# Three taps of a depthwise 3x3 convolution as diagonal matmuls on TensorE, among the windows of a window attention

## The reference

```
x = _ln2d(x0, ln_w, ln_b)
x1 = lax.conv_general_dilated(x, dw_w, (1, 1), ((1, 1), (1, 1)), feature_group_count=c, ...) + dw_b
ca = _eca(x1, ...)                                  # gate per channel, from the mean of x1
q, k, v = three 1x1 convolutions of x; v is multiplied by ca
for each head (8 channels): windows of 8x8 pixels, shifted by 4; head 1's k and v are halved by a 2x2 convolution
    atn = softmax(q k^T * SCALE); y_ = atn v
x1m = sigmoid(sa_w y + sa_b) * x1
x = po_w (y + x1m) + po_b + x0
# second layer: 27 offset/mask maps by a 3x3 convolution, bilinear samples at 9 moved taps,
# a 1x1 sum over taps and channels, batch norm, relu, + x
```

## Time and profile before

| | |
|---|---|
| median of 3 runs | 899.45 us (898.77 to 900.86) |
| the profiled execution: its time, its span | 900.16 us, 898.4 us |
| TensorE busy with matmuls (PE) / loading weights (PEld) | 753.2 us / 567.2 us |
| VectorE (DVE), ScalarE (ACT), GpSimd (POOL) busy | 689.3, 583.7, 512.6 us |
| mean granted clock of TensorE, as a share of 2.4 GHz | 0.867 |

### The profile page before, as it was taken

The page is one execution under the profiler, slowest core; times in us unless marked ns, Lnnn a source line. Parts: engine busy times, 40 slices in busy tenths (PEclk is TensorE's granted clock), DMA queues, the critical chain, the costliest instruction groups (busy, mean ns, idle before and its releaser), DMA issues.

```text
span 898.4 us, 30646 instructions
## 1 busy us (share of the span) xinstructions
PE 753.2 (84%) x12794; PEld 567.2 (63%) x12794; DVE 689.3 (77%) x935; ACT 583.7 (65%) x1057; POOL 512.6 (57%) x345
## 2 busy tenths in 40 slices
PE   5989999999889996888888888888787887777753
PEld 1348888888734564766666667667576766555543
DVE  2486655665442121999999999999999999999975
ACT  2675555554411334989698888888778888778714
POOL 3031111110032000899889999999889899999960
PEclk9985555555579998999999999999999999999987
DMA  4000000000028204856555556565555556555402
GB/s 156 1 1 1 2 1 1 2 2 1 1 58 211 58 18 105 200 144 164 144 145 152 149 146 159 145 167 143 148 144 154 143 150 155 153 158 159 110 4 93
DMA packets 29951, 90.90 MB, mean 101 GB/s; under 512 B 10622, under 2 KB 10750, under 8 KB 29566
## 3 DMA queue, kind: packets, MB, share of 16 engines
q1 hardware_dynamic: 26672, 88.12, 37.1%
q10 hardware_dynamic: 3150, 0.88, 0.5%
HBM read 79.01 MB, written 3.28 MB: 92 GB/s over the span
## 4 chain that ended last, share of the span: by engine, by line
DVE 45%; PE 41%; issue 9%; ACT 2%; DMA 1%; POOL 1%; ACTq 0%; SPq 0%; DVEq 0%; POOLq 0%
PE PS L1109 36%; DVE region L759 29%; DVE region L771 13%; PE PS L1204 4%; DVE region L566 1%; PE PS L1223 1%; DMA region<-px_scratch 1%; DMA cst<-in_consts 0%; ACT region L866 0%; DVE region L563 0%; DVE region L552 0%; DVE region L543 0%; ACT region L1103 0%; ACT region L872 0%; DVE ecab L692 0%
## 5 line engine op out<-in xcount | busy, mean ns | idle before, releaser
L1109 PE MATMUL PS<-region 64*64 64x144 f32 (+2 forms) x10368 | 465.1, 302 | 96.7 <-issue 78.1
L1109 PEld LDWEIGHTS PS<-region 64*64 64x64 f32 (+2 forms) x10368 | 363.5, 143 | 190.7 <-issue 183.7
L759 DVE TENSOR_TENSOR region<-PS,region 128x864 f32<-128x864 f32 x384 | 380.8, 1044 | 12.9 <-PE PS L1109 12.9
L500 POOL TENSOR_TENSOR region<-region 128x768 f32<-128x768 f32 x128 | 202.4, 1581 | 66.3 <-DVE region L759 66.2
L504 POOL TENSOR_TENSOR region<-region 128x864 f32<-128x864 f32 x128 | 224.0, 1750 | 20.1 <-DVE region L759 1.7
L987 ACT ACTIVATE region<-region 128x1152 f32<-128x1152 f32 x128 | 149.2, 1165 | 34.3 <-PE PS L1109 30.4
L984 ACT ACTIVATE region<-region,cst 128x1152 f32<-128x1152 f32 x128 | 159.2, 1244 | 5.9 <-DMA region<-px_scratch 4.7
L771 DVE TENSOR_REDUCE region<-region 128x32 f32<-128x960 f32 x128 | 145.6, 1138 | 1.5 <-POOL region L504 1.5
L1109 PE MATMUL PS<-wg,xp 64*64 64x144 f32 x1024 | 82.0, 286 | 6.1 <-issue 6.1
L1018 ACT ACTIVATE region<-x,cst (+2 forms) x288 | 86.7, 413 | 0.0
L427 POOL TENSOR_TENSOR region<-region,cst 128x1024 f32<-128x1024 f32 x8 | 15.9, 1993 | 116.7 <-PE PS L1109 116.7
(11 more groups left out here) (113 smaller groups left out, 538.6 us busy)
## 6 DMA issues: line engine op xcount, KB each, us to landing
region<-px_scratch SPq DMA_DIRECT2D x256, 288.0 KB, 4.3
out<-region SPq DMA_DIRECT2D x4, 512.0 KB, 3.0
region<-xp SPq DMA_DIRECT2D x8, 140.2 KB, 2.9
region<-xp SPq DMA_DIRECT2D x8, 140.1 KB, 2.9
region<-xp SPq DMA_DIRECT2D x8, 140.0 KB, 2.9
cst<-in_consts SPq DMA_DIRECT2D x1, 1102.0 KB, 9.1
region<-xp SPq DMA_DIRECT2D x8, 132.0 KB, 2.7
region<-xp SPq DMA_DIRECT2D x8, 131.9 KB, 2.6
```

The lines of the kernel that those rows point to most:

```text
L500: pool.tensor_tensor(two_rows[:, :, :, 0:2 * THIRD - KEEP], two_rows[:, :, :, 0:2 * THIRD - KEEP], two_rows[:, :, :, KEEP:2 * THIRD], ALU. ...
L759: v.tensor_tensor(uu[:, 2 * u:2 * u + 2, :, THIRD * t:THIRD * (t + 1)], PS[:, 2 * t:2 * t + 2, 0:THIRD * C].rearrange("p h (a o) -> p h o ...
L1109: return nc.tensor.matmul(o, l, r, start=start, stop=stop)
```

## The change

Of the nine taps of `x1`'s blocks 1 to 7, three (the middle row of the kernel: centre, left, right) are made on TensorE, as matmuls with a diagonal 128x128 matrix of that tap's 128 weights, accumulated in PSUM. All nine taps of block 0 are made so. GpSimd builds the nine diagonal matrices `dd` in one multiplication of the identity with the tap weights (128x1152). TensorE makes block 0 in bank 6 between `scores(0)` and `values(0)`; after that each of the steps 0 to 27 makes two rows (128 pixels, three matmuls) in the free part of bank 7, after `probs(n - 1)`. ScalarE copies these two rows to `x1` with the bias (`conv_rows`, one per step), and for block 0 copies 512 pixels and sums them in one instruction. VectorE adds six taps instead of seven to each of the blocks 1 to 7, and none to block 0. ScalarE's `lead` and `lead_left` and GpSimd's addition are gone. Because ScalarE's copy of bank 7 may not run while TensorE writes there, that copy now waits for the three matmuls (`cv_ready`), and the next transposes wait for `conv_rows` (`cv_out`).

```
             pool.wait_ge(k_in, 16)
+            pool.tensor_tensor(dd, mid(ident, KK), end(w_("dw"), P), ALU.mult).then_inc(dd_ready, 1)
...
-                    pool.wait_ge(lead_step, 2 * i + 2)
-                    rows = x13[:, WS * (i + 1):WS * (i + 2), 1:W]
-                    pool.tensor_tensor(rows, rows, tap1, ALU.add).then_inc(lead_ready, 1)
...
-            parts = (range(2, 4), range(4, 6), range(6, 8), range(8, 9))
-            four_steps(0, (range(0, 3), range(3, 5), range(5, 7), range(7, 9)))
+            parts = (range(3, 4), range(4, 6), range(6, 7), range(7, 9))
+            four_steps(0, ((), (), (), ()))
...
                 a.activation(pts[:, u, 0:4, :].rearrange("p t k -> p (t k)"), PS[:, 6, :], ACT.Copy).then_inc(pt_out, 1)
+                act.wait_ge(cv_ready, min(n + 1, 27) + 2)
                 a.activation(pts[:, u, 4, :], PS[:, 7, 0:P], ACT.Copy).then_inc(pt_out, 1)
...
+            def conv_rows(n):
+                act.wait_ge(cv_ready, n + 2)
+                a.activation(x13[:, WS + 2 * n:WS + 2 * n + 2, :], PS[:, 7, P:2 * P].rearrange("p (r c) -> p r c", c=W), ACT.Identity,
+                             bias=w_("dw_b")).then_inc(cv_out, 1)
...
-            lead(1)
-            lead_left(1)
+            act.wait_ge(cv_ready, 1)
+            a.activation(x1[:, 0:CH], PS[:, 6, :], ACT.Identity, bias=w_("dw_b"), accum_out=small[:, 49:50]).then_inc(cv_out, 1)
...
-                if jj == 0 and 1 <= i < NWR - 1:
-                    lead_left(i + 1)
...
-                if jj == 3 and i < NWR - 2:
-                    lead(i + 2)
                 if 1 <= n <= 32:
                     probs(n - 1, (n - 1) % 2)
+                if n < 28:
+                    conv_rows(n)
...
             def probs(n, u):
                 pe.wait_ge(exp_ready, done(n))
                 pe.wait_ge(pt_out, 2 * n + 4)
-                if n == 0:
-                    pe.wait_ge(q_out, done(NCH - 1))
+                pe.wait_ge(cv_out, min(n + 1, 28) + 1)
...
+            def conv_taps(out, row, rows, which):
+                for t in which:
+                    dy, dx = TAPS[t]
+                    above = int(row == 0 and dy < 0)
+                    ca, cb = max(0, -dx), W - max(0, dx)
+                    ins = mm(out.rearrange("p (r c) -> p r c", c=W)[:, above:, ca:cb], dd[:, 3 * (dy + 1) + dx + 1, :],
+                             xe3[:, row + above + dy:row + rows + dy, ca + dx:cb + dx], start=t == which[0], stop=t == which[-1])
+                ins.then_inc(cv_ready, 1)
             for n in range(35):
                 if n < 32:
                     scores(n, n % 2)
+                if n == 0:
+                    pe.wait_ge(dd_ready, 1)
+                    pe.wait_ge(q_out, done(NCH - 1))
+                    conv_taps(PS[:, 6, :], 0, WS, range(KK))
                 if 2 <= n <= 33:
                     attend(n - 2, n % 2)
                 if 1 <= n <= 32:
                     probs(n - 1, (n - 1) % 2)
+                if n < 28:
+                    conv_taps(PS[:, 7, P:2 * P], WS + 2 * n, 2, range(ON_PE))
```

More of the change, by code:

```diff
@@ L184, in build @@
         sm = cut2(2 * 3 * 2 * B).rearrange("p (u t k) -> p u t k", u=2, t=3)
+        dd = cut2(KK * P).rearrange("p (t k) -> p t k", t=KK)
         cut2(None)
@@ L219, in build @@
         py4 = py.rearrange("p (r g k) -> p r g k", g=PAIRS, k=KK)
-        tap1 = two[:, 0, 0:WS * (W - 1)].rearrange("p (r c) -> p r c", c=W - 1)
         kv4 = kv.rearrange("p (w t k) -> p w t k", t=2, k=K2)
@@ L312, in stream @@
             pair(PAIRS - 1, True, chunks)
+        TAPS = [(0, 0), (0, -1), (0, 1)] + [(dy, dx) for dy in (-1, 1) for dx in (-1, 0, 1)]
+        ON_PE = 3
         block = ctx.enter_context(nc.Block())
@@ L613, in normalise_heads @@
                                     end(sm[:, u, 2, B * hd:B * (hd + 1)], CS), ALU.mult).then_inc(on_ready, 1)
-            taps = [(0, 0)] + [(dy, dx) for dy in (-1, 0, 1) for dx in (-1, 0, 1) if (dy, dx) != (0, 0)]
             def conv_taps(which, i):
-                first, last = i == 0, i == NWR - 1
-                before = 0 if first else (KK - 2) * i
                 for t in which:
-                    dy, dx = taps[t]
+                    dy, dx = TAPS[t]
                     wcol = w_("dw")[:, 3 * (dy + 1) + dx + 1:3 * (dy + 1) + dx + 2]
-                    above, below = int(first and dy < 0), int(last and dy > 0)
+                    below = int(i == NWR - 1 and dy > 0)
                     ca, cb = max(0, -dx), W - max(0, dx)
[L627 to L630, removed]
-                    else:
[L632 to L637, removed]
+                    src = xe3[:, WS * i + dy:WS * (i + 1) + dy - below, ca + dx:cb + dx]
+                    dst = x13[:, WS * i:WS * (i + 1) - below, ca:cb]
+                    if t == ON_PE:
+                        dve.wait_ge(cv_out, 4 * i + 1)
+                    else:
+                        dve.wait_ge(conv_step, (KK - ON_PE) * (i - 1) + t - ON_PE)
+                    v.scalar_tensor_tensor(dst, src, wcol, dst, ALU.mult, ALU.add).then_inc(conv_step, 1)
             def four_steps(i, parts):
@@ L658, in _ @@
                 normalise_heads(n, n % 2)
-            dve.wait_ge(conv_step, (KK - 2) * NWR + 2)
+            dve.wait_ge(conv_step, (KK - ON_PE) * (NWR - 1))
             v.reduce_sum(small[:, 48 + NWR:49 + NWR], x1[:, (H - WS) * W:], axis=AX.X).then_inc(eca_step, 1)
             dve.wait_ge(eca_step, 1)
-            dve.wait_ge(x1_sum, NWR - 1)
+            dve.wait_ge(x1_sum, NWR - 2)
+            dve.wait_ge(cv_out, 1)
             v.reduce_sum(small[:, 0:1], small[:, 49:49 + NWR], axis=AX.X).then_inc(eca_step, 1)
@@ L932, in _ @@
             act.wait_ge(pads_ready, 6)
[L933 to L942, removed]
+            def conv_rows(n):
+                act.wait_ge(cv_ready, n + 2)
+                a.activation(x13[:, WS + 2 * n:WS + 2 * n + 2, :], PS[:, 7, P:2 * P].rearrange("p (r c) -> p r c", c=W), ACT.Identity,
+                             bias=w_("dw_b")).then_inc(cv_out, 1)
             def row_sum(i):
-                act.wait_ge(conv_step, (KK - 2) * (i + 1) + 2)
+                act.wait_ge(conv_step, (KK - ON_PE) * i)
                 rows = x1[:, i * CH:(i + 1) * CH]
                 a.activation(rows, rows, ACT.Copy, accum_out=small[:, i + 49:i + 50]).then_inc(x1_sum, 1)
-            lead(1)
-            lead_left(1)
+            act.wait_ge(cv_ready, 1)
+            a.activation(x1[:, 0:CH], PS[:, 6, :], ACT.Identity, bias=w_("dw_b"), accum_out=small[:, 49:50]).then_inc(cv_out, 1)
             for n in range(36):
@@ L958, in _ @@
                     write(n - 4, WS * (i - 1) + SHIFT, 16 * jj + SHIFT)
-                if jj == 0 and 1 <= i < NWR - 1:
-                    lead_left(i + 1)
-                if jj == 0 and 1 <= i < NWR:
+                if jj == 0 and 2 <= i < NWR:
                     row_sum(i - 1)
```

3 lines of the change are left out of this document (2 added, 1 removed).

## The result

The median went from 900.15 us (4 runs, 898.77 to 902.42) to 857.57 us (4 runs, 844.39 to 868.15), a ratio of 0.943 (95% interval 0.933 to 0.954). This ratio, like those of the experiments, leaves out executions more than 1.5% above the fastest of their kernel (here 860.67 and 868.15 us); with all four it is 857.57/900.15 = 0.953. Timed again, the changed kernel took 853.22 us (6 runs, 845.62 to 855.76; the kernel before 898.39 beside it), ratio 0.950 (0.947 to 0.953). None of these is left out, so this is the better estimate. The profiled execution took 854.47 us with a span of 852.7 us, 45.7 us less than the one of before. The changed kernel's first executions spread over 24 us, those of before over 4; in later series it was 10 us against 6 to 8.

The account below looks back on a forecast made before the run. TensorE bounds the attention, at half clock. First transposes at 67.4, 27 steps of 3.7, last four 18.4, then 4.8: 190.5 instead of 244.4; 900.16 - 53.9 = 846.3 profiled, median 845.5 us, range 830 to 912.

Parts of the forecast that it names:

- slower rival: Attention steps with taps: clock drops to 1.2 GHz and stays, each step 5.81 + 1.26 us, 930 to 950 us; chance 0.18.
- the clock being lost for a part of the steps: Attention: 3 to 15 steps at 1.2 GHz, 856 to 896 us; a few more and it's slower; chance 0.12.
- the case of the held clock: Attention: clock stays at 2.4 GHz and TensorE bounds, 832 to 864 us, likeliest 845.5; chance 0.60.
- The block-0 taps: Start of attention: 18 instructions take 7.9 us at 2.4 GHz; first transposes at 67.4 instead of 60.54, 6.9 us later.
- at the place of the fall: Start of attention, clock fell between 57 and 59.7 us: 7 to 8 us of dense full-array work put exactly there.
- The period: One attention step with taps at 2.4 GHz: 3.7 us, bounds 3.4 and 4.1, over 27 steps.
- TensorE: 5.81/2: Attention step: TensorE's present 5.81 us halves at 2.4 GHz; with 0.66 us of taps, 3.57 us.
- The check that was to bear it out: Scores' 16 instructions: 0.46 us to the next group at 2.4 GHz against 0.84 at 1.2, so halving is fair.
- The last steps: Last 4 attention steps, no taps: two at 3.4 us, two at 5.81, together 18.4 us.
- Never comes back: Attention steps with taps: once the clock goes to 1.2 GHz it stays there, 5.81 + 1.26 us per step.
- ScalarE's loop: Attention: ScalarE's 2.98 us plus two waits on TensorE make steps about 4.5 us, 860 to 878 us; chance 0.09.
- The rule that transposes don't count: Attention: transposes, a quarter of a step, do nothing to hold the clock; by it, 1.2 GHz in every step.

Follow-up runs that it names:

- the first gap filled: Kernel with one tap of block 0 on TensorE, plus three unread 128x512 matmuls behind step 0's values, where TensorE waits for VectorE: 848.85 us, ratio 0.944.

## Why the prediction was right, and where it was off

**The bound and the mechanism** were right: TensorE bounds before and after, and the clock decides the sign. The run with useless matmuls shows the gain without any relief, and the runs with one matmul and with a quarter of the array show the slower rival's mechanism. That the latter's 941.43 us is so near the rival's 940 is luck: the 940 hold 6.9 us for block 0, which that run doesn't have, and 34 us for the added work, which cost 41.

**The size**: 846.3 us predicted for the profiled execution, 854.47 measured, 8.2 us more; for the median 845.5, against 857.57 and 853.22. The attention ended 8.8 us later than predicted, and what follows took 0.6 us less. The sum had no step with taps at 1.2 GHz. Two of the first four executions (860.67 and 868.15) and their median lie in the range that the prediction gave to the clock being lost for a part of the steps, 856 to 896, so what came is the case of the held clock with some of that rival in it.

**The block-0 taps**: 7.9 us predicted, 7.58 measured; the first transposes at 67.4, measured 66.29. Of those 1.1 us, 1.0 is that the taps began at 55.49 and not 56.50; this start moves by more between executions (53.78 in the changed kernel's second profile), so it isn't a gain of the change. `dd` on GpSimd took 2.37 us (2.4 predicted). The staging of values behind it ended 0.6 us after the first scores' start, where it ended 1.5 ahead of it before: 2.1 us later, which the block-0 taps covered as predicted. The prediction also laid weight on dense work *at the place of the fall*. It neither suffices (ratio 0.998 to 1.005 alone) nor is necessary (848.32 us with the matmuls in the steps and none there, 844.86 with one tap).

**The period** is the term that was mis-sized: 3.7 us predicted, 3.99 measured, 27 x 0.29 = 7.8 us of the 8.8 us by which the attention ended later than predicted (199.3, not 190.5). The taps were right (0.66, measured 0.67) and so was `back`. The step that failed is "TensorE: 5.81/2": the small matmuls went from 4.34 only to 2.52 us, not 2.17, and the transposes from 1.26 to 0.69, not 0.63. The check that was to bear it out compared unlike things: 0.46 us is from the scores' start to the next group's, 0.84 the duration of a group. Like with like, gives 0.53 against 0.84, or 0.46 against 60.47 - 59.70 = 0.77 (the transposes' start by the timeline): about 0.6, as was then measured. In the changed kernel's last steps the same instructions stand at both levels:

```profile
178.27 1.64 PE L1097 MATMUL PS<-region 32*64 32x160 f32 x36
186.65 2.79 PE L1097 MATMUL PS<-region 32*64 32x160 f32 x36
```

That is 0.59. Two further terms: two steps of 5.6 and 5.2 us around the fall at 98 us, 2.8 us more, and the first transposes 1.1 us early.

**The last steps**: predicted 18.4 us for the four without taps, with the clock falling midway; measured 194.48 - 176.59 = 17.9. The rest behind the attention: predicted unchanged, measured 0.6 us less.

**"Never comes back"** was wrong as a statement on the mix with three taps: in the profiled execution the clock fell at 98 us and was up again at 103. That makes the rival of a partial loss mild; it shows as spread.

**ScalarE's loop** didn't close: its second copy waited for the taps once, 0.7 us. VectorE's wait for the scores, predicted under 0.5 us a step, was about 0.8 us a step (20.1 us in 26 steps); VectorE's own work there, 81.09/26 = 3.12 us, was as predicted (3.15), so the longer period is what it waited out.

**The rule that transposes don't count** was given weight as the slower rival. The run with six added transposes gave 849.54 us and a granted clock of 1.00; the row that seemed to speak for the rule had six in a step at 0.50, with nothing else dense beside them. The Trainium skill states the rule in "TensorE: Matmul & The Clock Gate", "Part 4: PE-mode transpose"; this run contradicts it for f32 transposes. The same page's section "Why this matters for your kernels" has the rule that keeping TensorE busy brings the full clock; it is contradicted by three kernels with 170 to 190 us of busy time without a gap, by the profile's modelled ends, at 0.50: the one before, the one with one matmul and the one with a quarter of the array.

## What to carry to other kernels

Where the profile shows TensorE fully busy and the granted clock at 0.50, don't read it as a bound by work alone: look at how much of the array the matmuls fill, and try a little full-array work beside them, useful if there is some, useless otherwise; here 0.67 us of it per step of 5.81 us made the step 3.99 us. Too little of it was a plain loss (1.012 with one matmul), and with two or three taps the executions spread, so time several and compare the granted clock of each. A busy time measured at 1.2 GHz shouldn't be halved for 2.4 GHz: of streams of small matmuls 58% was left here, not 50%.

## What the hardware showed that was not expected

Work whose result nobody reads made the kernel 5% faster. Full-array and quarter-array matmuls of the same columns differ by 10% in the kernel's time, nearly all of it through the clock. The run with f32 transposes held the clock as that with matmuls did.

The one fall in the middle of the changed kernel's first profile comes after a stretched step. VectorE's halving tap (L567) took 2.17 us while GpSimd's multiplication (L431) ran; of the changed kernel:

```profile
92.97 2.17 DVE L567 SCALAR_TENSOR_TENSOR region<-region,wr 128x256 f32<-128x256 f32 x1
```

```profile
92.64 2.21 POOL L431 TENSOR_TENSOR region<-region,cst 128x1024 f32<-128x1024 f32 x1 [14.01 <-PE PS L1097]
```

In the kernel before, that instruction takes 475 ns in the median of 24; the longest, 2158, stands at 50.58 us, also beside GpSimd's multiplications (ns, min/median/max):

```profile
L566 DVE SCALAR_TENSOR_TENSOR region<-region,wr x24: 472/475/2158, 40.3 to 96.5; 128x256 f32<-128x256 f32 x24
```

Behind it (transposes at 94.00, 99.64 and 104.80 us, so steps of 5.6 and 5.2) TensorE, in the changed kernel, waited 0.59 us for VectorE and 0.47 us for ScalarE, and the clock fell at the end of that step:

```profile
97.08 0.53 PE L1097 MATMUL PS<-region 32*64 32x160 f32 x16 [0.59 <-DVE region L599]
98.07 0.32 PE L1097 MATMUL PS<-region 128*64 128x18 f32 x3 [0.47 <-ACT region L904]
```

```profile
99.64 1.26 PE PS L1191 x5
...
104.80 0.70 PE PS L1191 x5
```

The second profile of the same changed kernel (845.62 us) has the same stretched step and the same two waits, but the clock didn't fall: VectorE's taps, TensorE's wait, the next transposes (0.77 us, not 1.26), and the window.

```profile
90.87 2.56 DVE L567 SCALAR_TENSOR_TENSOR region<-region,wr 128x256 f32<-128x256 f32 x2
95.37 0.53 PE L1097 MATMUL PS<-region 32*64 32x160 f32 x16 [0.59 <-DVE region L599]
97.45 0.77 PE L1191 MATMUL PS<-cst,region 128*128 128x128 f32 x5
62.00:180.00 118.00, 115.25 (x1750) 98.09 (x1750) 92.91 (x249) 91.72 (x276) 11.95 (x6) 1.00 0.01 2
```

With one tap of block 0 the step is there too and the clock stayed up; with the first gap filled it is there (from 87.86 us) and the clock fell right behind it, at 94 to 96. The stretched step by itself costs 1.2 us (5.16 instead of 3.99), and in one and the same program the clock may or may not fall after it. These runs don't show what decides that, nor whether it would fall without the step: none took GpSimd's multiplication away.
